# Decoder kernel, expert layer: results scattered by names stored behind each row, and inputs turned one shared layer ahead of their routing

## What is computed

```python
def _moe(x, gate, expert_bias, w1, w2, w3, shared_w1, shared_w2, shared_w3):
    xt = x.reshape(-1, dim)                                  # 2048 x 512
    scores = jax.nn.sigmoid((xt @ gate.T).astype(jnp.float32))   # 8 experts
    _, sel = jax.lax.top_k(scores + expert_bias[None, :], 2)
    top_scores = jnp.take_along_axis(scores, sel, axis=1)
    ...
    routed = xt[token_idx] * scores_sorted[:, None]          # 4096 rows, by expert
    xb = routed.astype(jnp.bfloat16)
    for e in range(NUM_EXPERTS):
        h = jax.nn.silu(xb @ w1e.T) * (xb @ w3e.T)
        oe = (h @ w2e.T)
        out_r = out_r + jnp.where((expert_ids == e)[:, None], oe, 0.0)
    hs = jax.nn.silu(xt @ shared_w1.T) * (xt @ shared_w3.T)
    out = hs @ shared_w2.T
    out = out.at[token_idx].add(out_r)
    ...
x = _layernorm(x + moe(x))
```

## Time and profile before

| | us |
|---|---|
| three timed runs, median (lowest, highest) | 2942.64 (2941.36, 2946.05) |
| the profiled execution, device time | 2947.47 |
| its span in the profile | 2945.7 |
| busy in the span: TensorE, VectorE, ScalarE, GpSimd | 2639.9, 1988.5, 1464.4, 1199.9 |
| routing and shared expansions of the last stage | 2674 to 2796 |
| blocks of the experts | 2796 to 2872 |
| adding up and normalising | 2872 to 2936 |
| last store and end | 2936 to 2945.7 |

### The profile page before, as it was taken

The page is one execution under the profiler, slowest core; times in us unless marked ns, Lnnn a source line. Parts: engine busy times, 40 slices in busy tenths (PEclk is TensorE's granted clock), DMA queues, the critical chain, the costliest instruction groups (busy, mean ns, idle before and its releaser), DMA issues. The chain is left out here.

```text
span 2945.7 us, 47353 instructions
## 1 busy us (share of the span) xinstructions
PE 2639.9 (90%) x16941; PEld 1760.8 (60%) x16941; DVE 1988.5 (68%) x2542; ACT 1464.4 (50%) x2868; POOL 1199.9 (41%) x1106
## 2 busy tenths in 40 slices
PE   8999899888888888886999899999997889997886
PEld 5666645534444444443999777777775555556653
DVE  4788757689999999966112079999999733333353
ACT  3444413289999998862222166666666311112410
POOL 0000025446666565542222058688888500001304
PEclk9999999989999999997999999999999999997898
DMA  2123513269888887964002221011112271111163
GB/s 97 65 77 116 201 51 100 77 133 168 170 170 163 170 172 162 191 154 159 32 29 74 100 79 45 26 55 58 51 51 94 77 129 36 43 66 58 61 151 118
DMA packets 534873, 296.52 MB, mean 101 GB/s; under 512 B 438160, under 2 KB 482192, under 8 KB 530832
## 3 DMA queue, kind: packets, MB, share of 16 engines
q1 hardware_dynamic: 518720, 260.31, 35.1%
q0 software_dynamic: 15952, 33.56, 4.0%
HBM read 126.43 MB, written 62.78 MB: 64 GB/s over the span
## 5 line engine op out<-in xcount | busy, mean ns | idle before, releaser
L1181 DVE TENSOR_REDUCE xh_top<-xh_seen 128x1 f32<-128x512 f32 (+1 forms) x768 | 631.3, 863 | 46.0 <-PE xh_seen L1083 32.5
L1153 ACT ACTIVATE xh_prob<-xh_sc,xh_bias,xh_scale 128x1024 int16<-128x1024 f32 (+1 forms) x512 | 609.8, 1201 | 69.5 <-PE xh_sc L1083 69.3
L2328 POOL TENSOR_TENSOR ss_state<-ss_du,ss_b_all 128x1024 f32<-128x1024 f32 x128 | 445.7, 3495 | 169.4 <-PE ss_turned L1926 97.8
L1083 PE MATMUL xh_seen<-xh_kT,xh_qT 96*128 96x512 bf16 x1024 | 354.0, 387 | 81.8 <-DVE xh_top L1181 79.8
L2376 DVE TENSOR_TENSOR_SCAN ss_state<-ss_decay,ss_state 128x1024 f32<-128x1024 f32 x128 | 387.3, 3027 | 27.3 <-ACT ss_decay L2178 27.3
L1083 PE MATMUL xh_sc<-xh_kT,xh_qT 96*128 96x512 bf16 x1024 | 309.0, 384 | 1.3 <-ACT xh_prob L1153 1.3
L1207 POOL CAST xh_probT<-xh_pairs 128x2048 int16<-128x2048 uint8 x128 | 241.8, 1889 | 11.3 <-DMA xh_pairs<-xh_prob 2.7
L1083 PEld LDWEIGHTS xh_seen<-xh_kT,xh_qT 96*128 96x128 bf16 x1024 | 89.3, 97 | 242.8 <-DVE xh_top L1181 220.4
L1933 PE MATMUL ss_bank<-ss_xc,hold_w_conv 128*128 128x256 f32 x1024 | 229.3, 379 | 0.7 <-ACT ss_xc L2190 0.7
L2178 ACT ACTIVATE ss_decay<-ss_delta,ss_a 128x255 f32<-128x255 f32 x512 | 210.7, 496 | 0.4
L1933 PEld LDWEIGHTS ss_bank<-ss_xc,hold_w_conv 128*128 128x128 f32 x1024 | 190.0, 189 | 26.4 <-ACT ss_xc L2190 1.1
(11 more groups left out here) (392 smaller groups left out, 4886.5 us busy)
## 6 DMA issues: line engine op xcount, KB each, us to landing
ex_rows_in<-sa_zeros POOLq DMA_DIRECT2D x18, 1024.0 KB, 6.7
ss_b_all<-ss_states SPq DMA_DIRECT2D x8, 2048.0 KB, 7.2
xa_kT<-xp_kT SPq DMA_DIRECT2D x8, 768.0 KB, 5.3
xh_qT<-xa_qT SPq DMA_DIRECT2D x48, 128.0 KB, 3.2
xh_kT<-xa_kT SPq DMA_DIRECT2D x48, 128.0 KB, 3.3
ex_rows_out<-ex_oe SPq DMA_DIRECT2D x23, 256.0 KB, 2.2
sa_x<-in_x SPq DMA_DIRECT2D x8, 512.0 KB, 3.6
sa_y<-in_x SPq DMA_DIRECT2D x8, 512.0 KB, 10.9
```

Of the source, the lines that this page charges most:

```text
L1083: ins = pe.matmul(out[:, c * D:(c + 1) * D], qT[s][:, t * P:(t + 1) * P], kT[s][:, at + c * D:at + (c + 1) * D], start=True, stop=True)
L1153: act.activation(out, scores, ACT.Exp, bias=bias[t % RING][:, :], scale=scale[s][:, t:t + 1], accum_out=total[s][:, half, t:t + 1]).then_i ...
L1181: ins = v.tensor_reduce(top[t % RING][:, k:k + 1], scores[:, 0:n], AX.X, ALU.max)\
L2328: g.tensor_tensor(state[k % RING][:, :, :], du[s][:, :, :], spread(b_all[s][:, k, :], KD), ALU.mult)\
```

## The change

Three things are done at once.

*Names behind the data.* A row of `rows_in` is 544 numbers wide instead of 512 (1088 bytes); behind the data stands, as a 32-bit number, the row of a new DRAM tensor `results` into which the row's result goes: 2 x token + choice for a row with a token, and 4096 + its own number for a row without. The filling in the first stage writes these numbers, with an iota on GpSimd ahead of each transfer, and each transfer waits for the one before. For rows with a token GpSimd writes them into `xs` with an iota per layer.

*Blocks scatter.* For each block SyncE loads the 256 names (`name`) and, as before, the rows with a transposing DMA, now into one of four tiles; it no longer stores results. GpSimd scatters each block's result, two indirect transfers of 128 rows, to the rows named. VectorE's `plan` loses the part that found each token's result rows (6 operations), and packs the experts of 8 blocks into one number, so that TensorE loads 3 numbers into registers instead of 23 and takes a block's expert out of one with a shift and a mask. When all scatters have landed, SyncE loads the two results of each token with one plain load per layer, into buffers that the normalising then overwrites.

*Turning ahead.* `turn_input` of a layer stands one shared expansion earlier on TensorE, and ScalarE's `front` likewise. The count of the last layer goes to another PSUM bank (`xin`) and no longer waits for the placing of the layer before.

```diff
-            chunks = hold.rows_in.rearrange("(p r) d -> p (r d)", p=P).rearrange("p (c n) -> p c n", n=zeros.shape[-1])
+            chunks = hold.rows_in.rearrange("(p r) d -> p (r d)", p=P).rearrange("p (c n) -> p c n", n=UNUSED * ROW)
             for n in range(B - 1):
                 inverse_root(g, ln, n)
                 for c in range(3 * n, min(3 * n + 3, chunks.shape[1])):
-                    g.dma_start(chunks[:, c, :], zeros[:, :]).then_inc(hold.zeroed, 16)
+                    g.wait_ge(unused_set, ONE + c + 1)
+                    if c > 0:
+                        g.wait_ge(hold.zeroed, 16 * c)
+                    g.iota(unused[:, :, D:D + 2].bitcast(mybir.dt.int32)[:, :, 0], [[1, UNUSED]],
+                           base=2 * T + c * UNUSED, channel_multiplier=EXPERT_ROWS // P).then_inc(unused_set, 1)
+                    g.wait_ge(unused_set, ONE + c + 2)
+                    g.dma_start(chunks[:, c, :], flat(unused[:, :, :])).then_inc(hold.zeroed, 16)
...
-                at = sp.value_load(table[0:1, 0, j:j + 1], min_val=0, max_val=EXPERT_ROWS - S)
+                at = sp.value_load(rows_at[0:1, j:j + 1], min_val=0, max_val=EXPERT_ROWS - S)
                 if j == 0:
                     for s in (0, 1):
                         sp.wait_ge(scattered[s], 16 * 2 * TB * B // 2)
-                if j >= 3:
-                    sp.wait_ge(up_ps, ONE + B + j - 2)
-                sp.dma_start_transpose(rowT[j % 3][:, :, :], rows_in[bass.ds(at, S), :]).then_inc(row_loaded[j % 3], 16)
-
-            for j in range(3):
+                if j >= 4:
+                    sp.wait_ge(up_ps, ONE + B + j - 3)
+                rows = rows_in[bass.ds(at, S), :]
+                sp.dma_start(name[:, j, :, :], rows[:, NAME].rearrange("(t p) o -> p t o", p=P),
+                             allow_slow_non_contiguous=True).then_inc(block_loaded[j % 4], 16)
+                sp.dma_start_transpose(rowT[j % 4][:, :, :], rows[:, 0:D]).then_inc(block_loaded[j % 4], 16)
+
+            for j in range(BLOCKS):
                 load_rows(j)
-            for j in range(BLOCKS):
-                if j + 3 < BLOCKS:
-                    load_rows(j + 3)
-                sp.wait_ge(oe_ready, ONE + j + 1)
-                sp.dma_start(block_rows(rows_out, j * S), oe[j % 3][:, :, :]).then_inc(oe_stored[j % 3], 16)
+            for i in range(3):
+                sp.wait_ge(oe_sent[i], 16 * TB * ((BLOCKS - 1 - i) // 3 + 1))
+            for n in range(B):
+                sp.dma_start(result[n], results[n * 2 * S:(n + 1) * 2 * S, :]
+                             .rearrange("(t p c) d -> p t (c d)", p=P, c=2)).then_inc(got[n], 16)
             for n in range(B):
                 sp.wait_ge(y_done, ONE + n + 1)
-                sp.dma_start(tokens(x_out, n), y_out[n % 2][:, :, :]).then_inc(stored[n % 2], 16)
-            for s in (0, 1):
-                sp.wait_ge(stored[s], ONE + 16 * (B // 2))
+                sp.dma_start(tokens(x_out, n), y_out[n][:, :, :]).then_inc(stored, 16)
...
             for n in range(B):
+                if n >= 2:
+                    g.wait_ge(scattered[n % 2], 16 * 2 * TB * (n // 2))
+                g.iota(xs[n % 2][:, :, :, NAME].bitcast(I32)[:, :, :, 0], [[1, 2], [2 * P, TB]], base=2 * S * n,
+                       channel_multiplier=2).then_inc(named, 1)
+                g.wait_ge(named, ONE + n + 1)
                 g.wait_ge(placed, ONE + n + 1)
                 g.wait_ge(xs_ready, ONE + n + 1)
...
-            g.wait_ge(result_placed, ONE + 1)
-            for i in range(3):
-                g.wait_ge(oe_stored[i], ONE + 16 * ((BLOCKS - 1 - i) // 3 + 1))
-
-            def gather(n):
-                if n >= PAIRS:
-                    g.wait_ge(y_ps, ONE + n - PAIRS + 1)
-                for i in (0, 1):
-                    for t in range(TB):
-                        g.indirect_dma_start(result[n][:, i, t, :], None, rows_out,
-                                             bass.IndirectOffsetOnAxis(ap=result_place[:, n, i, t:t + 1], axis=0))\
-                            .then_inc(got[n % PAIRS], 16)
-
-            gather(0)
+            for j in range(BLOCKS):
+                g.wait_ge(block_loaded[j % 4], ONE + 32 * (j // 4 + 1))
+                g.wait_ge(oe_ready, ONE + j + 1)
+                for t in range(TB):
+                    g.indirect_dma_start(results, bass.IndirectOffsetOnAxis(ap=name[:, j, t, :].bitcast(U32), axis=0),
+                                         oe[j % 3][:, t, :], None).then_inc(oe_sent[j % 3], 16)
             for n in range(B):
-                if n + 1 < B:
-                    gather(n + 1)
                 inverse_root(g, ln, n)
...
-                pe.wait_ge(placed, ONE + n)
+                if n < B - 1:
+                    pe.wait_ge(placed, ONE + n)
+                else:
+                    pe.wait_ge(xT_sb, ONE + B)
...
+
...
+                return [pe.value_load(experts_at[0:1, i:i + 1], min_val=0, max_val=E ** PER_WORD - 1) for i in range(WORDS)]
+
+            def expert(j):
+                return pe.snap((words[j // PER_WORD] >> (3 * (j % PER_WORD))) & (E - 1), min_val=0, max_val=E - 1)
...
+            turn_input(2)
             expand_shared(0)
-            turn_input(2)
             pe.wait_ge(made, ONE + 1)
             count_earlier(0)
             route(2)
+            turn_input(3)
             count_earlier(1)
-            turn_input(3)
             route(3)
+            turn_input(4)
             expand_shared(1)
             for n in range(2, B - 2):
                 count_earlier(n)
-                turn_input(n + 2)
                 route(n + 2)
+                if n + 3 < B:
+                    turn_input(n + 3)
                 expand_shared(n)
             count_earlier(B - 2)
...
             expand_shared(B - 2)
-            e = expand_shared(B - 1, between=choose_experts)
+            expand_shared(B - 1)
+            words = load_experts()
             pe.wait_ge(e_loaded, 48)
+            before_that = None
             for j in range(BLOCKS):
-                expand(j, e[j])
+                e = expert(j)
+                expand(j, e)
                 if j >= 1:
-                    contract(j - 1, e[j - 1])
-            contract(BLOCKS - 1, e[BLOCKS - 1])
+                    contract(j - 1, before_that)
+                before_that = e
+            contract(BLOCKS - 1, before_that)
...
+            front(2)
             gate_shared(0)
-            front(2)
             scale(0)
             odds(2)
+            front(3)
             scale(1)
-            front(3)
             odds(3)
+            front(4)
             gate_shared(1)
             for n in range(2, B - 2):
-                front(n + 2)
                 scale(n)
                 odds(n + 2)
+                if n + 3 < B:
+                    front(n + 3)
                 gate_shared(n)
```

121 lines of the change are left out of this document (59 added, 62 removed).

## The result

The changed kernel took 2924.38 us (median of 4 runs, 2923.55 to 2926.31), the kernel before 2943.78 (4 runs, 2941.36 to 2946.05) beside it: a ratio of 0.9934, with an interval of 0.992 to 0.9949. The forecast was 2921.9, range 2912.5 to 2934. A later group of runs gave 2948.02 (11 runs) against 2944.84 (ratio 1.0012, 1.0002 to 1.0022), while the kernel before took 2943.8 to 2945.2 in all five groups. Both results hold; what differs is told with the first experiment. Until then the profile is that of the first group, whose execution took 2926.31 us (span 2924.0).

A forecast was written before the change was run, and what follows sets the result against it. The prediction took a chain of waits in the last stage (routing, way to the first block, blocks, tail) to set its length. Savings of 11.8 + 3.8 + 5.1 = 20.7 us from 2942.64 gave 2921.9 us, range 2912.5 to 2934.

The forecast's parts named there:

- forecast A: Whole kernel: the time comes out as summed, 2918 to 2926 us, small terms going a few us either way; chance 0.55.
- Turning one layer earlier: Routing in the last stage: 1.18 us waits go in four rounds; VectorE's product of layer 5 comes 5.3 us earlier.
- rival C: Faster than summed: clock not lowered in the rounds, iota hidden, step 2.85, tail 6 us: 2913 to 2918; chance 0.10.
- To the first block: Last stage up to the first block's matmuls: block 0 starts 11.8 us earlier (10 to 14), the turning's gain included.
- Blocks: First to last block: steps of 2.95 us, 64.5 us instead of 68.3, so 3.8 less (6 less to 3.5 more).
- The widening: Transposing loads in the blocks: rows 1088 B apart would cost 1.75 us per transpose instead of 1.27; one way to rival B.
- Tail: Normalising at the end: without gathers on GpSimd the last pass ends at 2930.7 instead of 2935.87, 5.1 us less.
- First stage: Filling of the row buffer, 23 to 37 us per layer on GpSimd: costs nothing in the middle, up to 2 us in all.
- GpSimd falling behind VectorE: Blocks: sign that the forecast is wrong, GpSimd lagging so that the copies wait for their buffers; no size given.

The follow-up runs named there:

- the first experiment: The changed kernel timed again without edits, in the first group of experiments, against the kernel before: 2948.02 us, ratio 1.0012.
- before_packed: Kernel before with only the experts' numbers packed eight to a word, three register loads behind the last shared expansion instead of 23 between its matmuls: 2939.68 us, ratio 0.9979.
- three_rows: Changed kernel with three row buffers instead of four, all else as changed: 2941.20 us, ratio to the kernel before 0.9987.

## Why the prediction was right, and where it wasn't

The time was right, for the group it was first timed in: forecast A, 2.5 us off, with errors of both signs behind it.

*Turning one layer earlier: the term of 5.3 us was 2.3.* The sentence that failed is "I reckon the expansion of layer 1 to start 1 us later than before". It started 7.5 us later after the stage's first turning (2713.04 - 2670.56 = 42.5, before 35.0). The turning of layer 2 was moved ahead of the first shared expansion, and I took its input for loaded. SyncE issues that load at 2686.48, behind the last store of the stage before, and the turning starts 3.7 us after it; the first expansion, 9.5 us where nothing stands ahead of it, used to cover that. Put back, it gave 7.5 us. The rounds were better than said (7.7 us), bounded by VectorE and ScalarE as forecast (10.06 for 9.8); TensorE's expansions in the rounds take 7.07 us, a full clock that I had left to rival C.

*To the first block: 11.8 was 9.1,* 3.0 of it the error above; the other terms nearly cancel. Term by term: first scatter 6.0 us behind the product (5.5), the iota and its wait 0.2 (1.0), landing 1.4 (1.4), names 0.41 (0.5), first load to block 0, names included, 3.92 (3.8). before_packed shows the largest piece alone: the register loads, 7.4 us.

*Blocks: 3.8 was 4.6,* steps of 2.83 for 2.95, 1.06 us of waiting for the second load for 0.7, and a first expansion of 3.25 us for 1.85: the granted clock was 0.58 in it, after TensorE had stood idle for 5.81 us. That the steps got shorter because the store left SyncE's queue is argued and not shown: no run puts it back, and three_rows leaves out the fourth buffer only among pauses. SyncE's queue is 2.55 us per block (2779.45 to 2782.06 is the first, later ones 2789.95 to 2792.50) where I estimated 2.4. The widening that the Trainium skill's page "DMA: Bandwidth & Descriptors", section "How a descriptor splits into AXI transactions", states would, by the prediction's estimate from that page, have made 1.75 us of a transposing load at this pitch. The traces don't agree: they show 1.2 at 1088 B and 1.3 at 1280 B, where each row starts at a multiple of 256 B, so it decides nothing here.

*Tail: 5.1 was 5.2.* The result of layer 5 waits for TensorE as worked out (its statistics start 26.7 us after the first, as in the prediction), three results follow at once, and normalising then takes 4.03 us a layer. That this comes of the 32 gathers being gone is read from the waits; no run tests it alone.

*First stage: nothing,* as said: a fill lands in 5.1 us in the median (4.2 to 9.3), and three take 17 to 26 of the 40 us.

*Not in any rival:* the pauses behind the scatters. They turn 18 us into nothing in the first group of experiments. The range held because the first timing had none, and that was luck: 2948.02 in the next group lies far outside it. My sign for it, GpSimd falling behind VectorE, looked at the wrong thing: GpSimd's queue had room (2.53 of 2.83 us), it is TensorE's signals that came late. And 1.0 us at the very end, which I haven't traced.

## What to carry to other kernels

When an operation is moved ahead of another, ask what the other one was covering: the load of its input first. At an end in which one engine adds and another normalises, deal out the additions so that results come evenly: that order alone gave 7 to 10 us of tail here, more than the removal of 32 gathers. And a gain that rests on scatters running beside other engines' short steps is to be timed on more than one chip. Where an engine starts late though its operands seem ready, look up when the semaphore was raised before you blame that engine: the end of a matmul in the profile is modelled.

## What was not expected of the hardware

In three of five groups of runs (the four groups of experiments were on four chips), GpSimd's scatters of 128 rows of 1 KB, two per block, are followed by pauses in which VectorE or ScalarE waits for a signal of TensorE, 0.3 to 4.2 us longer than the modelled ends allow (14 to 21 times in 23 blocks, steps of 3.4 to 4.2 us instead of 2.8); in the profiles of the other two groups there was none. Each group had one chip, so whether it is the chip that differs isn't shown. Plain transfers of the same size from the same queue bring none. In SyncE's queue, an issue of a transposing load, 1.25 us long as a rule, takes 2.1 to 2.5 us at four places of the changed kernel's first profile, and in each of them a 16 KB transfer of the instruction queue starts.
